# Where the causal mask is applied: select operations of GpSimd on the staged relative products, or mask products of TensorE on the scores

## The reference

```python
q = (einsum('bsd,ed->bse', query, Wq) + bq)   # k and v alike, split into heads
QEr = jnp.einsum('bhsd,ld->bhsl', q, Er_s)    # relative products
Srel = _skew(QEr)                             # row i shifted left by S - 1 - i
attn = (QK + Srel) / math.sqrt(dh)
causal = jnp.tril(jnp.ones((S, S), dtype=bool))
attn = jnp.where(causal[None, None], attn, -jnp.inf)
attn = jax.nn.softmax(attn, axis=-1)
out = jnp.einsum('bhst,bhtd->bhsd', attn, v)
```

## Time and profile before

| | |
|---|---|
| median of 3 runs | 1283.88 us (1282.5 to 1286.7) |
| the profiled execution | 1286.1 us, of which the span from first to last instruction is 1284.6 us |
| mean granted TensorE clock, share of full speed | 0.91 |
| PE matmul busy | 1011.8 us, 79% of the span, 6434 instructions |
| PE weight load busy | 632.7 us, 49% |
| DVE busy | 696.2 us, 54%, 2140 instructions |
| ACT busy | 647.5 us, 50%, 1346 instructions |
| POOL busy | 223.0 us, 17%, 531 instructions |
| DMA | 227.41 MB, mean 177 GB/s; store and skewed load 64 times 640 KB each |

### The profile page before, as it was taken

One profiled execution on the slowest core, in us unless ns is written; L12 is line 12 of the kernel. 1 busy time (PEld: TensorE's weight loads), 2 busy tenths in 40 slices (PEclk: granted clock), 3 DMA queues, 4 the chain that ended last, 5 costly groups with the idle time before them and its releaser, 6 DMA issues. The chain is left out here.

```text
span 1284.6 us, 22764 instructions
## 1 busy us (share of the span) xinstructions
PE 1011.8 (79%) x6434; PEld 632.7 (49%) x6435; DVE 696.2 (54%) x2140; ACT 647.5 (50%) x1346; POOL 223.0 (17%) x531
## 2 busy tenths in 40 slices
PE   5746778788783746999999993355899999997487
PEld 3414444455452425999999992121333333334344
DVE  4735778888887621010101101475766666684597
ACT  2435777777772212333232331143677777763787
POOL 0000000000000360111111112701222222240232
PEclk9865999999996877999999997576999999998799
DMA  7478889999998657665666641345211111110001
GB/s 247 149 258 307 321 329 337 344 341 339 337 324 329 237 180 240 189 214 185 208 196 195 208 147 50 103 157 155 63 47 46 47 44 48 44 38 9 1 29 39
DMA packets 93319, 227.41 MB, mean 177 GB/s; under 512 B 9686, under 2 KB 51766, under 8 KB 87254
## 3 DMA queue, kind: packets, MB, share of 16 engines
q1 hardware_dynamic: 86454, 208.20, 46.5%
q0 software_dynamic: 6816, 18.62, 5.3%
HBM read 143.07 MB, written 83.62 MB: 176 GB/s over the span
## 5 line engine op out<-in xcount | busy, mean ns | idle before, releaser
L684 DVE CUSTOM_DVE_ANT_0 unused<-mpsS,mask_bias 128x512 bf16<-128x512 f32 x256 | 172.0, 691 | 82.8 <-PE mpsS L617 82.7
L711 ACT ACTIVATE mPT<-mpsB 128x512 f32<-128x512 f32 x256 | 152.6, 597 | 80.0 <-PE mpsB L624 73.7
L1358 ACT ACTIVATE hT<-ph,w 128x128 f32<-128x128 f32 x312 | 89.0, 368 | 198.0 <-PE ph L1332 198.0
L464 PE MATMUL psT<-ident,scores 128*128 128x128 f32 x640 | 108.6, 286 | 58.0 <-ACT scores L557 56.1
L1377 DVE TENSOR_TENSOR ys<-py,b 128x256 f32<-128x256 f32 x39 | 16.6, 425 | 249.3 <-PE py L1342 249.3
L512 DVE CUSTOM_DVE_ANT_0 scores<-psS,bias 128x512 f32<-128x512 f32 (+3 forms) x256 | 119.7, 487 | 53.1 <-DMA bias<-rel 45.1
L1332 PE MATMUL ph<-xT,w 128*128 128x128 f32 x1248 | 146.8, 276 | 0.0
L552 ACT COPY stage<-psE 128x512 f32<-128x512 f32 (+1 forms) x192 | 97.5, 510 | 97.6 <-DMA rel<-stage 70.8
L1332 PEld LDWEIGHTS ph<-xT,w 128*128 128x128 f32 x1248 | 143.7, 193 | 0.1
L1342 PE MATMUL py<-w,hT 128*128 x624 | 141.2, 379 | 0.7 <-DVE ys L1377 0.7
L557 ACT ACTIVATE scores<-scores,nm 128x128 f32<-128x128 f32 (+3 forms) x256 | 136.8, 566 | 5.2 <-DVE nm L525 5.2
(11 more groups left out here) (247 smaller groups left out, 1482.5 us busy)
## 6 DMA issues: line engine op xcount, KB each, us to landing
rel<-stage SPq DMA_DIRECT2D x64, 640.0 KB, 6.7
bias<-rel SPq DMA_DIRECT2D x64, 640.0 KB, 7.2
w<-in_w1p SPq DMA_DIRECT2D x39, 1028.0 KB
qk<-packed SPq DMA_DIRECT2D x64, 192.0 KB
mqk<-packed SPq DMA_DIRECT2D x64, 192.0 KB
w<-in_w2p SPq DMA_DIRECT2D x8, 1024.0 KB
slots_in<-zero_row SPq DMA_DIRECT2D x1, 4992.0 KB, 18.2
xs<-slots_in SPq DMA_DIRECT2D x39, 128.0 KB
```

Source lines behind the costliest of these rows:

```text
L464: tr = nc.tensor.transpose(psT[bank][:, to:to + P], scores[slot][:, at:at + P], ident[:, :])
L684: nc.vector.tensor_tensor_reduce(out=unused[:, i, :], in0=psS[i % 2][:, :], in1=mask_bias[:, i, :], scale=1.0, scalar=-3.0e38, op0=ALU.add ...
L711: nc.scalar.activation(PT[r][:, j, :], psB[j % 2][:, :], ACT.Exp, scale=1.0 / 4).then_inc(s_exp, 1)
```

## The change

Two GpSimd select instructions for each head now write -2^100 (NEG) into the unused triangle of each of the four tiles in stage, where p + c < 127, before the store. Each instruction covers two tiles, 128 by 256 elements. After the shift these are just the elements that land above the diagonal of the block before, so the addition of bias masks the scores. For the last tile the element right after the row's end is needed too: rows of stage and of rel get one more column (REL_P = 1281), set to NEG once by DVE. The store waits for the two selects (s_cut) in place of ACT's copies, and GpSimd's selects wait for ACT's copies. PE's four mask products of each head go. GpSimd's step now runs from step -8 on, the selects ahead of the spread in the same step; its wait for the cleared buffers moves to step 0. The skewed load's rows are now REL_P - 1 = 1280 elements apart, and 1280 long as before.

```diff
--- before.py
+++ after.py
@@ -62,7 +62,8 @@
 
     slots_in = dram("slots_in", (SLOT_TILES * P, D), F32)
     slots_out = dram("slots_out", (SLOT_TILES * P, D), F32)
-    rel = [dram(f"rel_{r}", (P, REL_W), F32) for r in range(RING)]
+    REL_P = REL_W + 1
+    rel = [dram(f"rel_{r}", (P, REL_P), F32) for r in range(RING)]
 
     with top:
         def sem(name):
@@ -388,7 +389,7 @@
             LOAD, REL, READ, SOFT, EXP = 8, 6, 4, 2, 1
             with ExitStack() as ctx:
                 qk = [sb(ctx, f"qk{r}", [KP, 2 * S], BF16) for r in range(ROUND)]
-                stage = [sb(ctx, f"stage{r}", [P, REL_W]) for r in range(2)]
+                stage = [sb(ctx, f"stage{r}", [P, REL_P]) for r in range(2)]
                 bias = [sb(ctx, f"bias{r}", [P, REL_W]) for r in range(RING)]
                 scores = [sb(ctx, f"scores{r}", [P, REL_W]) for r in range(RING)]
                 PT = [sb(ctx, f"PT{r}", [P, REL_W]) for r in range(ROUND)]
@@ -401,8 +402,8 @@
                 s_qk = [sem(f"s_qk{r}") for r in range(ROUND)]
                 s_wr = [sem(f"s_wr{r}") for r in range(RING)]
                 s_rd = [sem(f"s_rd{r}") for r in range(RING)]
-                names = ("emm", "eev", "smm", "soft", "nm", "exp", "tmm", "tev", "seen", "seensp")
-                s_emm, s_eev, s_smm, s_soft, s_nm, s_exp, s_tmm, s_tev, s_seen, s_seen_sp = (
+                names = ("emm", "eev", "smm", "soft", "nm", "exp", "tmm", "tev", "seen", "seensp", "cut", "edge", "seenpool")
+                s_emm, s_eev, s_smm, s_soft, s_nm, s_exp, s_tmm, s_tev, s_seen, s_seen_sp, s_cut, s_edge, s_seen_pool = (
                     sem(f"s_{n}") for n in names)
                 block = ctx.enter_context(nc.Block())
 
@@ -420,11 +421,13 @@
                             sp.sem_inc(s_seen_sp, 1)
                             wait(sp, s_soft, NU * (m - RING + 1))
 
-                            skewed = bass.AP(rel[slot].ap().tensor, P - 1, [[REL_W - 1, P], [1, REL_W]])
+                            skewed = bass.AP(rel[slot].ap().tensor, P - 1, [[REL_P - 1, P], [1, REL_W]])
                             sp.dma_start(bias[slot][:, :], skewed).then_inc(s_rd[slot], 16)
                         if h := stage_of(n, r, it, REL):
                             m, slot, turn = h
-                            sp.wait_ge(s_eev, NU * (m + 1))
+                            sp.wait_ge(s_cut, 2 * (m + 1))
+                            if isinstance(n, int) and n == -REL:
+                                sp.wait_ge(s_edge, 2)
                             wait(sp, s_rd[slot], 16 * turn)
                             sp.dma_start(rel[slot][:, :], stage[slot % 2][:, :]).then_inc(s_wr[slot], 16)
                         if isinstance(n, int) and n + READ == NBH:
@@ -447,11 +450,8 @@
                         bank = (NU * slot + u) % 2
                         wait(pe, s_soft, NU * m + u - 1)
                         for i, off, w in units[u]:
-                            nc.tensor.matmul(psS[bank][:, off:off + w], q_k[:, i * P:(i + 1) * P],
-                                             q_k[:, S:S + w], start=True, stop=False)
-
-                            mm = nc.tensor.matmul(psS[bank][:, off + w - P:off + w], identb[:, :], dmask[:, :],
-                                                  start=False, stop=True)
+                            mm = nc.tensor.matmul(psS[bank][:, off:off + w], q_k[:, i * P:(i + 1) * P],
+                                                  q_k[:, S:S + w], start=True, stop=True)
                         mm.then_inc(s_smm, 1)
 
                     def turn_probs(m, slot, u):
@@ -489,6 +489,8 @@
 
                 @block.vector
                 def _(dve):
+                    for rows in stage:
+                        nc.vector.memset(rows[:, REL_W:REL_P], NEG).then_inc(s_edge, 1)
                     vals.clear(dve)
 
                     def step(n, r, it):
@@ -527,12 +529,22 @@
 
                 @block.gpsimd
                 def _(pool):
-                    pool.wait_ge(vals.s_zero, 3)
+                    keep = dict(base=-(P - 1), channel_multiplier=1, compare_op=ALU.is_ge, fill=nc.gpsimd.to_reg(NEG))
 
                     def step(n, r, it):
+                        if h := stage_of(n, r, it, REL):
+                            m, slot, turn = h
+                            rows = stage[slot % 2]
+                            pool.wait_ge(s_eev, NU * (m + 1))
+                            pool.sem_inc(s_seen_pool, 1)
+                            for first in (rows[:, 0:1024].rearrange("p (u c) -> p u c", c=512)[:, :, 0:P],
+                                          rows[:, 896:1280].rearrange("p (u c) -> p u c", c=P)[:, 0:2, :]):
+                                nc.gpsimd.affine_select(out=first, in_=first, pattern=[[0, 2], [1, P]], **keep).then_inc(s_cut, 1)
+                        if isinstance(n, int) and n == 0:
+                            pool.wait_ge(vals.s_zero, 3)
                         if r % GROUP == 0 and (h := group_of(n, r, it, 0)):
                             vals.spread_values(pool, *h)
-                    run_heads(pool, 0, NBH - 1, step)
+                    run_heads(pool, -LOAD, NBH - 1, step)
 
                 @block.scalar
                 def _(act):
```

## The result

The changed kernel takes 1293.38 us (median of 4 runs, 1292.45 to 1295.02) against 1284.16 us for the kernel before (4 runs): the ratio is 1.0071, 95% interval 1.0051 to 1.0092. It is slower by 9.2 us. The forecast was no change, 1284.2 us, in a range from 1278 to 1306: the time lies inside the range and 9.2 us off the forecast, more than the 3.9 us that were called distinguishable.

A forecast was written before the change was run, and what follows sets the result against it. The prediction took the DMA queue to bound the kernel. Its terms, -1.0 + 1.3 + 0 = +0.3 us on the profiled 1286.1 us, gave 1286.4, for the median 1284.2 us (no change), range 1278 to 1306.

The forecast's parts named there:

- What bounds it: Steady part: the DMA queue, always holding something, sets the pace of 4.45 us per head; no compute engine is full.
- The cover of 3.0 us: Store's landing, 6.7 us against 3.7 when quieter: about 3.0 us is queueing that hides a later store.
- Rival A: Ring of two heads, not the queue: each head pays half of 1.3 us, 36 us, so 1321 us; chance 0.08.
- Edit 1: PE's four mask products go: 0 at full clock, -1.0 us over three heads at half clock; bounds 0 and -2.2.
- Rival C: PE stays at half clock longer, three more heads at 6.0 instead of 4.45 us: +4.7, 1289 us; chance 0.05.
- Edit 2: Two GpSimd selects, 0.60 us each, delay the store 1.3 us: steady cost 0, +1.3 us once at the start.
- rival D: Selects outlast the cover; at 2.5 us each, 0.95 us more for 55 heads: +52, 1336 us; chance 0.03.
- Edit 3: GpSimd's queue and shared port: DVE's small operation (L525) held 0.4 to 1.0 us per head, effect on time 0.
- Edit 4: Stored rows of 5,124 in place of 5,120 bytes: value 0, bounds 0 and +0.4 us per head.
- Rival B: Store slower on its odd rows: 0.3 to 0.4 us times 55 heads, 16 to 22 us, 1301 to 1306; chance 0.13.
- The sum: Whole kernel: -1.0 + 1.3 + 0 = +0.3 us, median forecast 1284.2 us, no change (chance 0.61).

The follow-up runs named there:

- e2: Kernel before with PE's mask products left out and nothing in their place; ratio 1.003 to the kernel before, head 4.469 us.
- e4: Kernel before with the selects and their waits alone, rows of 5,120 bytes, mask products kept; ratio 1.0035 to the kernel before, head 4.475 us.
- e7: Kernel before with the store's rows of 5,124 bytes alone, skewed load's rows still 1,279 elements apart (wrong elements read); ratio 1.0046, head 4.544 us.
- e6: e4 with each pair of selects made twice, the store going 1.97 us after the copies; ratio 1.0133 to the kernel before, head 4.711 us.
- e9: Kernel before, unaltered, run and profiled again; ratio 0.999 to the kernel before, head 4.453 us.
- e5: Changed kernel, unaltered, timed again in another session; ratio 1.0092 to the kernel before, head 4.649 us.
- e1: Changed kernel with PE's four mask products per head put back; ratio 1.0083 to the kernel before, head 4.583 us.
- the first comparison: Changed kernel's first timing against the kernel before, 1293.38 against 1284.16 us; ratio 1.0071.
- e3: Kernel before with the extra column alone (rows of 5,124 bytes), products kept, no selects; ratio 1.0053 to the kernel before, head 4.540 us.
- e8: Kernel before with only the skewed load's rows 1,280 elements apart (wrong elements read), stores as before; ratio 1.0012, head 4.450 us.
- e10: Changed kernel with rel rows of 5,632 bytes, padding filled once at the start, 5,120 bytes stored per row; ratio 1.0041 to the kernel before.
- e11: Kernel before with unused products on PE while the pipeline fills; ratio 1.0005 to the kernel before.

## Why the prediction was right or wrong, point by point

**What bounds it**: right. The DMA queue sets the pace; e2 and e4 change PE's and GpSimd's work and move the head by 0.02 us each (4.469 and 4.475 for 4.451), within what one program shows, and e7 moves it by 0.09 with four bytes more in each row of stage and rel and no engine's work changed.

**The cover of 3.0 us**: wrong in size. I took the whole difference of two landing times, 3.7 and 6.7 us, as slack. e4 and e6 show that of a delay of 0.95 us nearly all is absorbed, of 1.95 us only 1.4. The 3.7 us belong to a stretch in which a head takes 6.0 us and the other transfers are done; at 4.45 us per head they still have to pass. That is my reading; no run separates it. The delay was within the true cover, so the step's value, nearly 0, came out right but with some 0.5 us to spare (1.4 less 0.95) and not the 1.7 us that I had counted on (3.0 less 1.3). Rival A fell for this delay, but its ring is real one pair of selects further.

**Edit 1**: -1.0 us was not to be seen. From the first to the ninth store it is 38.1 us before (87.78 to 125.86), 36.1 after (90.73 to 126.78), but 35.5 in e9, the kernel before again (88.30 to 123.75): the start of one program scatters by more than the gain. What came with the edit, and was not on my list, are the clock's dips; e5 (1.0092) against e1 (1.0083) and the first comparison (1.0071) put the edit's sum, on top of the others, near nothing (each of the three has an interval of 0.15 to 0.25% to either side); alone, in e2, it is a loss of 0.3%. Rival C named the clock and the wrong place: I looked for a longer half clock at the start (it was not longer, 0.61 after for 0.59 before as mean from 100 to 130 us), and it fell within the steady part instead. SP's timeline of the changed kernel around the dip from 242.90 to 246.30:

```profile
242.38 0.32 SPq L432 DMA_DIRECT2D rel<-stage  x1
...
247.83 0.32 SPq L432 DMA_DIRECT2D rel<-stage  x1
...
252.06 0.32 SPq L432 DMA_DIRECT2D rel<-stage  x1
...
256.28 0.32 SPq L432 DMA_DIRECT2D rel<-stage  x1
```

One head takes 5.45 us, the next two 4.23 and 4.22 where 4.5 is usual: part of it is caught up, and this dip costs 0.4 us. Worked out in the same way against three heads of 4.5, the others cost between nothing (280 us) and 0.8 us (297 us), so five of them some 2 us as an estimate.

**Edit 2**: selects 0.41 us each, not 0.60, a pair 0.77, with the hop 0.95 in place of 1.3 us. The start cost 1.1 us (1.3 forecast). The landing time fell to 5.9, not 5.4. The estimate for a tight loop drawn in the prediction from the Trainium skill (GPSIMD Engine Reference, "3.1 Elementwise — side-by-side cycle accounting"), 0.4 us, agrees with the select's 0.41; rival D fell.

**Edit 3**: the held operation didn't come. The operation, now L527, has a median of 0.16 us as before: it starts at 209.54, before the copies end and 0.25 us before the selects begin. I had put it behind them. The few long ones, up to 0.40 us, are there before and after. The effect on the time, none, was as said.

**Edit 4**: this is the step that failed. I set the odd rows at 0 and their upper bound at 0.4 us per head; e3 and e7 measure 0.09, and 0.09 times 64 is 5.8 of the 9.2 us. Rival B had the store's side of the queue and four times the price. The estimate of 5 us that the prediction drew from the Trainium skill (DMA: Bandwidth & Descriptors, "How a descriptor splits into AXI transactions") and left out of its sum lies nearest to what was measured. That is luck rather than agreement: the page speaks of bytes that are read, the cost came with the rows that are written, and for the load, which reads, no cost can be measured (e8; its interval would still hide 0.3%).

**The sum**: +0.3 forecast, +9.2 measured. Odd rows 5.8, start 1.1, selects in the steady part 1.5 (64 times 0.024, a difference that lies within one program's scatter), together 8.4. The dips' 2 us and what the missing products win elsewhere are not settled between themselves; e4's loss beyond 2.6 us and e2's 3.8 us aren't located either. The range held the time because it had been drawn up to rival B's 16 to 22 us; no value that the prediction gave to an edit or a rival is near 9 us.

## What to carry to other kernels

When a DMA queue bounds the loop, a change of some bytes in a tile's row length is an edit of the bound resource, to be priced by a run of its own: e10, which keeps the stored rows on their old boundary and puts the padding into memory once rather than into each transfer, lost half as much. Slack behind a queue is not the difference between a busy and a quiet landing time; a run with the delay doubled shows where it ends. An engine that isn't the bound can still lose its clock when work is taken off it, so such work is worth removing only if its place on the path was seen.

## What the runs showed of the hardware that I had not expected

With stores of 128 rows of 5,124 bytes to consecutive addresses a head in a full queue takes about 0.09 us longer than with rows of 5,120 (4.540 and 4.544 for 4.451 us), though a stored row itself takes only 2 ns longer; a read whose rows start 5,120 bytes apart, all 508 bytes past a step of 5,120, costs no more than one whose rows start 5,116 bytes apart (4.450). A GpSimd select on 128x256 elements in place takes 0.41 us, less than the one-input operation of that size, 0.48. TensorE's granted clock fell to 1.2 GHz for 3.4 us at a time in a steady loop after four products of a head had been taken away, and was 1.00 again with them put back (e1); kernels with the products had such a dip too, but one at most with a single pair of selects (e7, e11).
